# A cross-attention and feed-forward layer on one core: another order for the last stretch, and three steps of the key and value stage moved by a slot or two

## The reference

```
x = x + xattn(layernorm(x), ctx)        # hidden = layernorm(x)
  xattn: q = rmsnorm(hidden) @ w_q.T; k, v = ctx @ w_k.T, ctx @ w_v.T     (32 heads of 128)
         p = softmax(q k^T + position_bias, masked); hidden + (p v) @ w_out.T
x = x + ffn(layernorm(x))
  ffn:   r = softmax(xf @ gate_w.T)                                       (8 experts)
         ((xf * (r @ in_scale)) @ sign(weight).T) * (r @ out_scale) + bias
```

## Time and profile before

| What | Value |
|---|---|
| Median of 3 runs | 832.54 us |
| The profiled execution | 832.86 us |
| Its span | 831.1 us |
| TensorE busy | 825.4 us, 99% |
| VectorE busy | 617.8 us, 74% |
| ScalarE busy | 392.4 us, 47% |
| GpSimd busy | 306.0 us, 37% |
| Mean granted TensorE clock | 1.000 |

### The profile page before, as it was taken

How to read it: one execution, slowest core, us unless ns; L and a number is a source line. 1 busy time by engine, 2 the same in 40 slices (tenths; PEclk the granted TensorE clock), 3 DMA queues, 4 the chain that set the end, 5 groups by cost and what they waited for, 6 DMA issues and landing times.

```text
span 831.1 us, 12839 instructions
## 1 busy us (share of the span) xinstructions
PE 825.4 (99%) x4330; PEld 698.3 (84%) x4330; DVE 617.8 (74%) x1006; ACT 392.4 (47%) x1009; POOL 306.0 (37%) x279
## 2 busy tenths in 40 slices
PE   9999999999999999999999999999999999999998
PEld 8878888888888878888888888888888888888887
DVE  6867846778776796887778777777767877777765
ACT  6632512432441444544554554554554455456683
POOL 2103211022030044725445445544543544446046
PEclk9999999999999999999999999999999999999999
DMA  8364464673453759414134214314313422423002
GB/s 312 118 228 166 141 218 135 197 253 126 140 179 102 229 162 313 177 57 156 46 117 156 94 69 156 107 56 159 137 52 130 155 87 77 155 78 148 1 1 103
DMA packets 60880, 114.07 MB, mean 137 GB/s; under 512 B 5240, under 2 KB 39160, under 8 KB 55568
## 3 DMA queue, kind: packets, MB, share of 16 engines
q1 hardware_dynamic: 60384, 112.86, 39.6%
q10 hardware_dynamic: 432, 0.39, 0.1%
HBM read 77.58 MB, written 35.65 MB: 136 GB/s over the span
## 4 chain that ended last, share of the span: by engine, by line
PE 98%; DVE 1%; ACT 0%; issue 0%; DVEq 0%
PE out L1356 11%; PE out L1358 11%; PE out L1357 11%; PE proj L1356 10%; PE proj L1358 10%; PE proj L1357 10%; PE o L1474 7%; PE s L1455 7%; PE s L1356 4%; PE s L1358 4%; PE s L1357 4%; PE t L1463 3%; PE proj L1550 1%; PE proj L1551 1%; PE t L1502 1%; PE s L1433 1%
## 5 line engine op out<-in xcount | busy, mean ns | idle before, releaser
L946 ACT ACTIVATE probs<-probs,neg_max 128x128 f32<-128x128 f32 x256 | 99.7, 391 | 132.4 <-DVE neg_max L1201 132.4
L768 POOL TENSOR_TENSOR w_stage<-w_stage 128x256 f32<-128x256 f32 x30 | 27.6, 920 | 305.6 <-DMA w_stage<-in_wk 126.8
L780 POOL TENSOR_TENSOR w_lo<-w_stage,w_hi 128x512 fp32r<-128x512 f32 (+1 forms) x52 | 59.4, 1154 | 140.7 <-ACT w_hi L884 140.7
L1233 DVE TENSOR_TENSOR acc<-out,acc 128x512 f32<-128x512 f32 x100 | 68.4, 688 | 36.8 <-PE out L1358 36.3
L1356 PE MATMUL out<-wo_hi,o_hi 128*128 128x512 f32 x224 | 95.2, 425 | 0.0
L1356 PE MATMUL proj<-x_hi,w_hi 128*128 128x512 f32 x210 | 88.6, 422 | 0.0
L1358 PE MATMUL out<-wo_lo,o_hi 128*128 128x512 f32 x224 | 88.3, 394 | 0.0
L1357 PE MATMUL out<-wo_hi,o_lo 128*128 128x512 f32 x224 | 87.6, 391 | 0.0
L1358 PE MATMUL proj<-x_lo,w_hi 128*128 128x512 f32 x210 | 82.7, 394 | 0.0
L1357 PE MATMUL proj<-x_hi,w_lo 128*128 128x512 f32 x210 | 82.0, 391 | 0.0
L792 POOL TENSOR_TENSOR bias_mask<-bias_raw,mask_neg 128x512 f32<-128x512 f32 x64 | 77.6, 1222 | 10.2 <-DVE probs L1198 10.1
(11 more groups left out here) (363 smaller groups left out, 2137.4 us busy)
## 6 DMA issues: line engine op xcount, KB each, us to landing
k_spill<-ring SPq DMA_DIRECT2D x64, 256.0 KB, 2.8
v_spill<-ring SPq DMA_DIRECT2D x64, 256.0 KB, 2.2
big_stage<-in_wv SPq DMA_DIRECT2D x8, 1024.0 KB, 8.1
w_stage<-in_wq SPq DMA_DIRECT2D x32, 256.0 KB, 4.5
k_first<-k_spill SPq DMA_DIRECT2D x8, 1024.0 KB, 7.4
v_first<-v_spill SPq DMA_DIRECT2D x8, 1024.0 KB, 4.8
wo_raw<-in_wo SPq DMA_DIRECT2D x16, 512.0 KB, 3.3
k_second<-k_spill SPq DMA_DIRECT2D x8, 1024.0 KB, 6.9
```

Of the source, the lines that this page charges most:

```text
L780: pool.tensor_tensor(lo, staged(m, part), hi.bitcast(F32), ALU.subtract).then_inc(g_wlo, 1)
L946: last = act.activation(probs[:, j % 2, b, :], probs[:, j % 2, b, :], ACT.Exp, bias=neg_max[:, col:col + 1], accum_out=row_sum[:, col:col ...
L1233: dve.tensor_tensor(acc[:, b, :], bank_tensor[:], acc[:, b, :], ALU.add).then_inc(v_acc, 1)
```

## The change

- The step `S` is parted in two steps, `S` (TensorE) and `SC` (VectorE), so that a written order can set them apart. Wherever `S` stands in the lists that stay, both parts stand there.
- In the key and value stage `VX 0 3` goes from cycle 4, slot 0 to cycle 3, slot 5; `H 2` from slot 1 to slot 3 of its cycle; `XT T4` from slot 3 to slot 4 of its cycle.
- The written order now begins right after `OUT(15, 1)` and `ST 0`. The steps are the same as before; their order is another on each engine.

```
-PARTS_OF = {"T": ("T", "PT"), ...
+PARTS_OF = {"S": ("S", "SC"), "T": ("T", "PT"), ...
-    put(4, 0, ("WS", 3), ("VX", 0, 3))
+    put(3, 5, ("VX", 0, 3))
+    put(4, 0, ("WS", 3))
-    put(k - 4, 1, ("H", 2))
+    put(k - 4, 3, ("H", 2))
-    put(k + 5, 3, ("XT", "T4"))
+    put(k + 5, 4, ("XT", "T4"))
-    steps += swift(j + 5, [*outs(c, 1), ("ST", 0), *outs(c, 2), ("ST", 1)], outs(c, 3), [])
-    steps += slot(j + 6, [("ST", 2), ("ST", 3)], [("LN2", 0), ("ROOT", 0), *outs(b, 4)], outs(b, 5), [("LS", 0)], copy_first=True)
+    steps += [("S", j + 6), ("OUT", c, 1), ("ST", 0)]
     steps = [part for step in steps for part in parts_of(step)]
...
+    steps += [("OUT", 15, 2), ("T", 61), ("PT", 61), ("BM", 63), ("OUT", 15, 3), ("ADD", 15, 2), ("EXP", 62), ("ST", 2), ("S", 63),
+              ("ADD", 15, 3), ("PV", 61), ("SC", 63), ("OUT", 14, 5), ("OH", 61), ("N", 62), ("EXP", 63), ("OL", 61), ("T", 62), ("OUT", 14, 4),
+              ("ST", 1), ("PT", 62), ("ST", 3), ("PV", 62), ("LN2", 0), ("N", 63), ("ROOT", 0), ("OUT", 14, 6), ("OH", 62), ("LS", 0),
+              ("OL", 62), ("NT", 0), ("T", 63), ("PT", 63), ("TX", 0), ("NT", 1), ("PV", 63), ("TXC", 0), ("BI", 1), ("TX", 1), ("OH", 63),
+              ("GA", 0), ("TXC", 1), ("OL", 63), ("BI", 0), ("NT", 3), ("OUT", 15, 4), ("NT", 2), ("G", 0), ("TX", 2), ("GM", 0), ("ADD", 15, 4),
+              ("GE", 0), ("TX", 3), ("OUT", 15, 5), ("TXC", 2), ("ROUTE", 0), ("TXC", 3), ("ST", 4), ("BI", 3), ("GA", 1), ("ADD", 15, 5),
+              ("RT", 0), ("BI", 2), ("G", 1), ("ST", 5), ("RTC", 0), ("OUT", 14, 7), ("GM", 1), ("LN2", 2), ("GE", 1), ("ROUTE", 1), ("R", 0, 1),
+              ("R", 0, 0), ("Y", 0, 0), ("RT", 1), ("ROOT", 2), ("OUT", 15, 7), ("RTC", 1), ("LS", 2), ("YH", 0, 0), ("Y", 0, 1), ("NT", 5),
+              ("R", 1, 0), ("YL", 0), ("R", 1, 1), ("OUT", 15, 6), ("YH", 0, 1), ("Y", 1, 0), ("NT", 4), ("YP", 0), ("ADD", 15, 7), ("OS", 0),
+              ("YH", 1, 0), ("TX", 4), ("ADD", 15, 6), ("BI", 5), ("TX", 5), ("OSC", 0), ("Y", 1, 1), ("M", 0, 0), ("TXC", 4), ("ST", 7),
+              ("YH", 1, 1), ("BI", 4), ("OS", 1), ("GA", 2), ("ST", 6), ("OSC", 1), ("TXC", 5), ("LN2", 3), ("M", 0, 1), ("YL", 1), ("ROOT", 3),
+              ("G", 2), ("LS", 3), ("YP", 1), ("MP", 0), ("M", 1, 0), ("GM", 2), ("GE", 2), ("M", 2, 0), ("NT", 6), ("NT", 7), ("ROUTE", 2),
+              ("TX", 6), ("TX", 7), ("TXC", 6), ("SUM", 0), ("OS", 2), ("TXC", 7), ("RT", 2), ("M", 1, 1), ("RTC", 2), ("BI", 6), ("OSC", 2),
+              ("R", 2, 0), ("MP", 1), ("GA", 3), ("Y", 2, 0), ("BI", 7), ("OS", 3), ("M", 2, 1), ("YH", 2, 0), ("OSC", 3), ("YL", 2), ("G", 3),
+              ("SUM", 1), ("R", 2, 1), ("GM", 3), ("OS", 4), ("GE", 3), ("Y", 2, 1), ("M", 3, 0), ("ROUTE", 3), ("YH", 2, 1), ("M", 3, 1),
+              ("OSC", 4), ("MP", 2), ("YP", 2), ("RT", 3), ("MP", 3), ("M", 4, 0), ("RTC", 3), ("SUM", 2), ("R", 3, 1), ("R", 3, 0), ("OS", 5),
+              ("Y", 3, 0), ("M", 5, 0), ("OSC", 5), ("SUM", 3), ("Y", 3, 1), ("YH", 3, 0), ("OS", 6), ("M", 4, 1), ("YH", 3, 1), ("YL", 3),
+              ("OSC", 6), ("M", 5, 1), ("YP", 3), ("MP", 4), ("M", 6, 0), ("MP", 5), ("SUM", 4), ("M", 6, 1), ("SUM", 5), ("OS", 7), ("MP", 6),
+              ("M", 7, 1), ("OSC", 7), ("SUM", 6), ("M", 7, 0), ("MPL", 1), ("SUML", 1), ("MPL", 0), ("SUML", 0)]
```

More of the change, by code:

```diff
@@ L79, in bias_of @@
     return j // 2 if j < 2 * SPLIT else j - SPLIT
-PARTS_OF = {"T": ("T", "PT"), "PV": ("PV", "OH", "OL"), "OUT": ("OUT", "ADD"), "WO": ("WOH", "WOLO")}
+PARTS_OF = {"S": ("S", "SC"), "T": ("T", "PT"), "PV": ("PV", "OH", "OL"), "OUT": ("OUT", "ADD"), "WO": ("WOH", "WOLO")}
 def parts_of(step):
@@ L290, in schedule @@
     steps += swift(j + 4, outs(b, 3), outs(c, 0), [])
-    steps += swift(j + 5, [*outs(c, 1), ("ST", 0), *outs(c, 2), ("ST", 1)], outs(c, 3), [])
-    steps += slot(j + 6, [("ST", 2), ("ST", 3)], [("LN2", 0), ("ROOT", 0), *outs(b, 4)], outs(b, 5), [("LS", 0)], copy_first=True)
+    steps += [("S", j + 6), ("OUT", c, 1), ("ST", 0)]
     steps = [part for step in steps for part in parts_of(step)]
-    steps += [("T", 63), ("OUT", 14, 6), ("NT", 0), ("PT", 63), ("TX", 0), ("NT", 1), ("PV", 63), ("TXC", 0), ("BI", 1), ("TX", 1), ("OH", 63),
[14 rows of a table removed]
-              ("MPL", 1), ("SUML", 1), ("MPL", 0), ("SUML", 0)]
+    steps += [("OUT", 15, 2), ("T", 61), ("PT", 61), ("BM", 63), ("OUT", 15, 3), ("ADD", 15, 2), ("EXP", 62), ("ST", 2), ("S", 63),
[17 rows of a table added]
+              ("M", 7, 1), ("OSC", 7), ("SUM", 6), ("M", 7, 0), ("MPL", 1), ("SUML", 1), ("MPL", 0), ("SUML", 0)]
     return steps
@@ L1331, in _ @@
                   "CT": ctx_sum, "CX": ctx_low, "LN": input_statistics, "RMS": mean_squares, "RMSR": rms_reciprocals, "H": normed,
-                  "XT": x_sum, "XX": x_low, "MASK": masks, "S": scores, "N": normalise,
+                  "XT": x_sum, "XX": x_low, "MASK": masks, "SC": scores, "N": normalise,
                   "OL": out_low, "ADD": add_out, "ST": ffn_statistics, "LN2": ffn_norms, "LS": normal_scales, "NT": normal_tile,
```

## The result

The changed kernel takes 834.94 us (median of 8 executions, 833.84 to 837.24) against 832.43 for the kernel before (8 executions, 831.82 to 833.41): ratio 1.0031, 95% interval 1.0022 to 1.0041. That is slower by 0.3%. The forecast was 833.2 in a range of 831.6 to 834.9, and no change to be told. The profiled execution took 835.21 us, its span is 833.4, 2.3 over the span of before.

A forecast was written before the change was run, and what follows sets the result against it. TensorE was taken as the bound (busy 825.4 of 831.1 us). Small moves -1.0, order up to OUT 15.4 +1.9 and behind it -0.25 gave +0.65 on 832.54, so 833.2 us, range 831.6 to 834.9.

The forecast's parts named there:

- Loss 784.05 - 781.51 = 2.54: Last attention units: TensorE idles 2.54 us between PV61 and output product OUT 14.5, which waits for OL61 on VectorE.
- The order up to OUT 15.4: Last stretch up to output product OUT 15.4: losses of 3.4 us against 1.53 before, so +1.9 us.
- PV63's wait for PT63: Last attention unit: only TX0 stands between T63 and PV63, so PV63 waits for PT63's copy, 0.45 us lost.
- Behind OUT 15.4: From output product OUT 15.4 to the kernel's end: waits gone and new ones sum to -0.2 to -0.3 us.
- OS2's wait: Behind OUT 15.4: the three OS stand further apart, each copy is done in time, -0.58 us.
- RT1: Behind OUT 15.4: no OS stands before it and ROUTE1 ends 0.2 after it could start, +0.19 us.
- RT2: Behind OUT 15.4: it needs TX6's copy out of its bank, +0.2 us.
- OS7's move: End of kernel: OS7 after M 6,1 lets MPL 0 wait for the last matmul alone, -0.2 us.
- The small moves: Key and value stage: moving VX 0 3, H 2 and XT T4 closes three TensorE gaps, -1.0 us.
- that the wait doesn't bind: Rival: the wait before OUT 14.5 costs nothing, total change -3.3 us, 829.2 us; chance 8%.
- The normalised tiles: Rival: at TX0 they come late behind the root's table load, 1.2 us more, 834.4 us; chance 16%.
- That the small moves give nothing: Rival: moved parts are as late in their new places, -1.0 falls out, +1.65 us, 834.2 us; chance 8%.

The follow-up runs named there:

- the second set: The changed kernel measured again, nothing altered, beside the kernel before: 834.24 us (11 executions), ratio 1.0017.
- full-clock trace: Profiled execution of the unaltered changed kernel, measured again, in which the clock did not fall; that run's median is 834.24 us, ratio 1.0017.

## Why the prediction was wrong

- **The step that failed** is "Loss 784.05 - 781.51 = 2.54" in the part on the new order up to OUT 15.4. The gap was named at its place, with its cause and its length (measured 2.5). Its price was taken to be its length. In 10 of 19 executions it cost 1.64 us more, since the matmuls behind it ran for 3.4 us at the 1.2 GHz level. No rival had this; of the clock the prediction said nothing, although the profile shows it at 1.000 and so with only one way to go, and this was the one edit that left TensorE idle for longer than the trace of before ever does. How far off the median came to lie was luck: 6 of the 8 executions had the drop and put it 0.04 over the range, with 4 of 11 in the second set it was 834.24.
- **The order up to OUT 15.4, full clock:** +1.9 forecast. In the full-clock trace OUT 15.4 starts 2.0 later, relative to OUT 15.2, than before. PV63's wait for PT63 is there (0.25 shown idle, 0.4 from start to start; 0.45 forecast).
- **Behind OUT 15.4:** OS2's wait is gone. RT1 loses 0.12, RT2 0.26, M 4,0 0.24; 0.19, 0.2 and 0.15 were forecast. From OUT 15.4 to the last matmul the full-clock trace takes 36.10 where it was 35.98: 0.1 more, and 0.1 less was forecast. OS7's move works: MPL 0 starts 0.04 after the last matmul has ended, and no longer 0.25.

```profile
830.08 0.28 PE L1565 MATMUL proj<-x_hi,x_lo 128*128 128x256 f32 x1
830.40 0.42 DVE L1323 TENSOR_TENSOR k_first<-proj,v_second 128x256 f32<-128x256 f32 x1
```

- **The small moves:** all three gaps gone, as forecast, 1.0 us; the traces show 1.0 at the first PV. The medians show 0.6, with an interval that holds both. One more loss is seen at 306.52, 0.48 to the next start where it was 0.37 before, and single gaps of 0.2 fall at another place of the attention in each trace.
- **The rivals:** that the wait doesn't bind is wrong. The normalised tiles were in time: the table load takes 1.28 and the root follows it at once, so TX0 has no wait. That the small moves give nothing is wrong by the traces.

```profile
786.03 0.60 ACT L957 ACTIVATE probs_t<-t 128x512 f32<-128x512 f32 x1 [3.16 <-PE t L1466]
786.64 1.28 ACT L921 ACT_TABLE_LOAD   x1
787.94 0.20 ACT L921 ACTIVATE std<-var_eps 128x4 f32<-128x4 f32 x1
```

The Trainium skill (ScalarE: Activation LUTs, What ACT_TABLE_LOAD costs) has a drain of some 1.4 us with each switch to a different set. By that page the root would come at 789.3 (an estimate); it came at 787.94, and the load itself 0.01 after the copy before it had ended, so here the measurement decides.

The sum of the forecast, +0.65, is to be set beside the full-clock executions: their mean is 833.71, that of the 35 executions of the kernel before in both sets is 832.64, so +1.1. Of the 0.4 between, 0.3 is in the trace: 0.1 up to OUT 15.4 and 0.2 behind it. The rest of the distance to 834.94, 1.2, is the clock: 1.64 in 6 of 8.

Open stays when a gap of 2.3 us or more brings the clock down and when not: the same gap did both within one execution. What the runs show is the share of each length from 2.3 us on, not the rule.

## What to carry to other kernels

Price an idle gap of the bound engine by its length and, where it comes near the 2.3 us that brought the clock down here, by the clock as well: with 2.5 us it was 1.6 us more, in every second execution. It is seen neither in busy shares nor in waits, only in the granted clock of the stretch behind the gap and in matmul starts 0.42 apart. When an order is written out, look for a product that stands directly behind the last link of its own way through the other engines, and put independent work between; where there is none, put the step that the bound engine waits for first on the engine that is not the bound.

## What the runs showed of the hardware that was not expected

- After a gap of 2.5 us the clock fell 0.8 us *behind* the gap's end, in the midst of busy matmuls (783.66), and stayed down for 3.4 us. In the three other profiled executions with a drop it fell 0.4, 0.4 and 1.4 us behind the gap's end, and also for 3.4 us.
- Ten unused matmuls in the idle time delayed nothing, and none of 11 executions had the clock of 0.998.
- XT T4 took 1.76 us in its new place and 1.21 before, H 2's two halves 1.05 and 1.11 beside GpSimd's sums (0.96 and 1.11 before). The Trainium skill (SBUF — State Buffer, Who interferes with whom) has VectorE operations with two SBUF inputs blocked by a GpSimd operation that reads SBUF, which T4 fits (GpSimd busy from 293.14 for 0.93 us, T4 from 293.39). Before the change T4 started 0.04 ahead of GpSimd's operation, and it was that one which took long, 1.78. Nobody waited for either.
